# One 128x64 product for four heads' chunk states, four copies of its diagonal blocks, and a reordered projection

## The reference, cut to what matters

```python
def step(carry, inp):
    z, s = carry
    u_t, dt_t, k_t, Bz_t, Bx_t, Cz_t, Cx_t = inp
    dtE = dt_t[:, :, None, None]
    S = 1.0 / (1.0 + dt_t[..., None] * k_t[..., None] + (dt_t * dt_t)[..., None] * A)
    z = S[..., None] * (z - dtE * A[None, :, :, None] * s + dtE * (Bz_t[..., None] * u_t[:, :, None, :]))
    s = s + dtE * z + dtE * (Bx_t[..., None] * u_t[:, :, None, :])
    y = jnp.einsum('bhn,bhnd->bhd', Cz_t, z) + jnp.einsum('bhn,bhnd->bhd', Cx_t, s)
    return ((z, s), y)
```

## Time and profile before

| | us |
|---|---|
| median of 3 runs | 2338.43 (2335.57 to 2339.53) |
| profiled execution | 2331.21 |
| its span, first to last instruction | 2329.6 |
| VectorE busy in the span | 2050.5 (88%) |
| TensorE busy in the span | 1875.7 (81%) |
| ScalarE busy in the span | 1083.9 (47%) |

### The profile page before, as it was taken

The page is one execution under the profiler, slowest core; times in us unless marked ns, Lnnn a source line. Parts: engine busy times, 40 slices in busy tenths (PEclk is TensorE's granted clock), DMA queues, the critical chain, the costliest instruction groups (busy, mean ns, idle before and its releaser), DMA issues. The chain is left out here.

```text
span 2329.6 us, 78341 instructions
## 1 busy us (share of the span) xinstructions
PE 1875.7 (81%) x31266; PEld 1078.5 (46%) x31266; DVE 2050.5 (88%) x5467; ACT 1083.9 (47%) x1700; POOL 84.5 (4%) x28
## 2 busy tenths in 40 slices
PE   6777468987888898888888889887888898367886
PEld 3333134444444444444444444444444444246775
DVE  6887599999999999999989989998999998487774
ACT  4665235454444454445544444544545455034553
POOL 0000000000000000000000000000000000153300
PEclk9898779999999999999999999999999999578997
DMA  4555634655555565545655554665455543433400
GB/s 139 178 214 184 178 92 112 147 134 131 124 127 125 119 150 130 125 106 134 145 123 126 138 124 109 145 143 125 110 126 129 117 113 87 159 154 136 145 27 27
DMA packets 224663, 300.25 MB, mean 129 GB/s; under 512 B 96784, under 2 KB 114192, under 8 KB 218128
## 3 DMA queue, kind: packets, MB, share of 16 engines
q1 hardware_dynamic: 174416, 212.11, 35.9%
q10 hardware_dynamic: 48704, 78.68, 13.3%
q0 software_dynamic: 1152, 4.19, 0.5%
HBM read 240.85 MB, written 50.86 MB: 125 GB/s over the span
## 5 line engine op out<-in xcount | busy, mean ns | idle before, releaser
L670 PE MATMUL m_ps_a<-m_valT,m_w_bc 128*128 128x512 f32 x2048 | 962.1, 619 | 59.8 <-DMA m_valT<-scratch_valT 32.0
L670 PEld LDWEIGHTS m_ps_a<-m_valT,m_w_bc 128*128 128x128 f32 x2048 | 389.8, 198 | 491.1 <-issue 483.7
L958 DVE TENSOR_TENSOR m_prod<-m_psi,m_shear 128x128 f32<-128x128 f32 x960 | 369.0, 384 | 0.0
L962 DVE TENSOR_TENSOR m_psi<-m_psi,m_prod 128x128 f32<-128x128 f32 x960 | 368.4, 384 | 0.0
L818 ACT ACTIVATE m_sq<-m_ps_a 128x512 f32<-128x512 f32 x256 | 152.8, 597 | 372.4 <-PE m_ps_a L670 367.9
L833 ACT ACTIVATE m_kT<-m_ps_g 128x512 f32<-128x512 f32 x128 | 72.0, 596 | 249.8 <-PE m_ps_g L716 249.8
L716 PE MATMUL m_ps_g<-m_ident,m_k 128*128 128x128 f32 x512 | 88.9, 330 | 103.8 <-DVE m_k L1060 103.5
L695 PE MATMUL m_ps_g<-m_q,m_k 32*64 32x64 f32 x8192 | 122.8, 232 | 45.3 <-issue 38.9
L695 PEld LDWEIGHTS m_ps_g<-m_q,m_k 32*64 32x64 f32 x8192 | 107.5, 133 | 100.2 <-ACT m_dX L840 53.3
L819 ACT ACTIVATE m_raw<-m_ps_a 128x512 f32<-128x512 f32 x256 | 151.6, 592 | 0.0
L755 PEld LDWEIGHTS m_ps_y<-m_q,m_X 32*16 32x16 f32 x7168 | 105.2, 94 | 84.1 <-issue 84.1
(11 more groups left out here) (143 smaller groups left out, 3061.7 us busy)
## 6 DMA issues: line engine op xcount, KB each, us to landing
m_scale<-scratch_norm SPq DMA_DIRECT2D x256, 256.0 KB, 5.3
m_w_bc<-in_w_bcT ACTq DMA_DIRECT2D x252, 256.0 KB, 4.7
m_shear<-scratch_n_alpha SPq DMA_DIRECT2D x64, 256.0 KB, 5.3
m_shear<-scratch_beta SPq DMA_DIRECT2D x256, 64.0 KB, 4.1
m_det<-scratch_gd SPq DMA_DIRECT2D x256, 64.0 KB, 4.5
scratch_gateT<-gate SPq DMA_DIRECT2D x8, 1024.0 KB, 3.9
scratch_valT<-val SPq DMA_DIRECT2D x8, 1024.0 KB, 4.5
scratch_svgT<-svg SPq DMA_DIRECT2D x8, 1024.0 KB, 5.5
```

What stands on the lines that cost most here:

```text
L670: mm = pe.matmul(ps_a[j % 2].ap(), w_bc[:, j, kt, :], valT[:, kt, :], start=(kt == 0), stop=(kt == KI - 1), skip_group_check=True)
L958: dve.tensor_tensor(prod.ap(), psi_t[half][:, :, :, :, t], shear_t[half][:, :, :, t].unsqueeze(1).to_broadcast([P, 2, 2, HALF * NC]), ALU. ...
L962: ins = dve.tensor_tensor(psi_t[half][:, :, :, :, t + 1], psi_t[half][:, :, :, :, t], prod[:, :, ::-1, :], ALU.add)
```

## The change

The chunk states of four heads are made by one product per chunk and part: 128 columns of kT (all four heads' states) against 64 columns of u (all four heads' values). The result is 128x64, of which the four 32x16 blocks on the diagonal are the heads' states. All 8 chunks are made instead of 7. They lie in the upper half of all four banks of `ps_g` (`place`: even chunks in banks 0 and 2, odd ones in 1 and 3). ScalarE takes the blocks out with four copies, one for each head's 32 partitions, over four banks. `dX` holds the chunks in the order of `place`. In `inner`, product 0 stands whole ahead of the chunk states, and product 1 stands between them and the scores.

```diff
@@ -458,7 +458,7 @@
         kt = sb("kt", [P, 2, T])
         g = sb("g", [P, HP, PAIRS * C])
         kT = sb("kT", [P, 2, T])
-        dX = sb("dX", [P, NC - 1, 2, DH])
+        dX = sb("dX", [P, NC, 2, DH])
         X = sb("X", [P, NC - 1, 2, DH])
         cross = sb("cross", [P, 2, 2, DH])
         V = sb("V", [P, 2, DH])
@@ -470,11 +470,14 @@
         ps_g = ctx.enter_context(nc.psum_tensor("m_ps_g", [P, HP, T], F32))
         ps_y = ps("y")
 
-        def ps_dX(c):
-
-            col = PAIRS * C + c // 2 * 2 * DH
-            return ps_g[:, 2 + c % 2, col:col + 2 * DH].rearrange("p (r d) -> p r d", r=2)
-
+        def place(c):
+
+            return (c // 4 * 2 + c % 2) * 2 + c // 2 % 2
+
+        def ps_dX(c, part):
+
+            bank, col = place(c) // 2, PAIRS * C + (place(c) % 2 * 2 + part) * HP * DH
+            return ps_g[:, bank, col:col + HP * DH]
 
         consts_in = sem("consts_in")
         const_set = sem("const_set")
@@ -698,13 +701,11 @@
                         mm.then_inc(g_made.sem, g_made.step)
 
                 def chunk_states(s, c):
+
                     for part in range(2):
-                        for h in range(HP):
-                            heads = slice(c // 2 * P + h * N, c // 2 * P + (h + 1) * N)
-                            mm = pe.matmul(ps_dX(c)[h * N:(h + 1) * N, part, :], kT[rows_of(c), part, heads],
-                                           u[rows_of(c), s, c // 2, h * DH:(h + 1) * DH], start=True, stop=True,
-                                           skip_group_check=True)
-                    if c == NC - 2:
+                        mm = pe.matmul(ps_dX(c, part), kT[rows_of(c), part, c // 2 * P:(c // 2 + 1) * P],
+                                       u[rows_of(c), s, c // 2, :], start=True, stop=True, skip_group_check=True)
+                    if c == NC - 1:
                         mm.then_inc(dX_made.sem, dX_made.step)
 
                 def transpose_k(b, group):
@@ -721,20 +722,19 @@
 
                     s = group % 2
                     if ahead:
-                        product(b, group + 2, 0, (0, 1, 2))
+                        product(b, group + 2, 0, range(KI))
                     pe.wait_ge(kT_ready.sem, kT_ready.at(b, group * 2 + 1))
                     pe.wait_ge(u_in[s].sem, u_in[s].at(b, group // 2))
                     pe.sem_inc(passed, 1)
-                    for c in range(NC - 1):
+                    for c in range(NC):
                         chunk_states(s, c)
                     if ahead:
-                        product(b, group + 2, 0, (3,))
+                        product(b, group + 2, 1, range(KI))
                     pe.wait_ge(dX_ready.sem, dX_ready.at(b, group))
                     pe.wait_ge(q_ready.sem, q_ready.at(b, group))
                     for c in range(NC):
                         scores(s, c)
                     if ahead:
-                        product(b, group + 2, 1, range(KI))
                         product(b, group + 2, 2, range(KI))
 
                 def inner_outputs(s, odd):
@@ -835,11 +835,11 @@
                 def copy_dX(b, group):
                     act.wait_ge(dX_made.sem, dX_made.at(b, group))
                     act.wait_ge(X_ready.sem, X_ready.at(b, group * (NC - 1) - 1))
-                    for odd in range(2):
-                        count = NC // 2 - odd
-                        ins = act.activation(dX[:, odd:NC - 1:2].rearrange("p c r d -> p c (r d)"),
-                                             ps_g[:, 2 + odd, PAIRS * C:PAIRS * C + count * 2 * DH
-                                                  ].rearrange("p (c e) -> p c e", c=count), ACT.Copy)
+                    for h in range(HP):
+                        rows, cols = slice(h * N, (h + 1) * N), slice(h * DH, (h + 1) * DH)
+                        ins = act.activation(dX[rows].rearrange("p (k i) r d -> p k (i r) d", k=HP),
+                                             ps_g[rows, :, PAIRS * C:].rearrange("p k (i c) -> p k i c", i=HP)[:, :, :, cols],
+                                             ACT.Copy)
                     ins.then_inc(dX_ready.sem, dX_ready.step)
 
                 def store_y(b, group):
@@ -1095,7 +1095,7 @@
                         dve.wait_ge(y_made.sem, y_made.at(b, group - 1))
                         for c in range(NC - 1):
                             if c:
-                                dve.tensor_tensor(V.ap(), dX[:, c], X[:, c - 1], ALU.add).then_inc(own.sem, own.one())
+                                dve.tensor_tensor(V.ap(), dX[:, place(c)], X[:, c - 1], ALU.add).then_inc(own.sem, own.one())
                                 v_made = own.n
                                 advance(1)
                                 dve.wait_ge(own.sem, v_made)
```

## The result

| | before | after |
|---|---|---|
| median of the runs, us | 2337.0 (4 runs) | 2500.19 (2495.32 to 2504.69, 4 runs) |
| ratio, 95% interval | | 1.0698 (1.0668 to 1.0728) |
| span of the profiled execution, us | 2329.6 | 2494.5 |
| mean granted TensorE clock | 0.913 | 0.888 |

What follows compares the result with a forecast made beforehand. VectorE, in program order, was taken to bound the kernel; dX 4.03 us later per group gave 89 + 136 us, less 10 and 15, plus 10: +210 us, so 2548 us, range 2440 to 2640.

Steps and rivals of the forecast that it cites:

- one-for-one rule: First m_cross on VectorE: each microsecond dX comes later than VectorE is ready costs the kernel one, once per group.
- Rival E: First m_cross: the change doesn't reach VectorE because slack grows with the period; about 2338 us, chance 0.03.
- Product 0 whole in front: TensorE ahead of the chunk states: its last quarter, two records, delays dX by 0.86 us, double at half clock.
- The chunk states: TensorE: 32 records paced by 128-column weight loads take 3.5 us instead of 1.13, so dX comes 2.37 us later.
- rival D: Chunk states: both row halves side by side, 1.1 us, and TensorE keeps full clock; kernel faster, 2300 us, chance 0.04.
- its own sign of being wrong: The prediction called itself wrong if chunk states took 2 us or less, or VectorE didn't wait at first m_cross.
- Rival A: Chunk states: the 64 moving columns set the pace in single file, 2.1 us; 2458 us, chance 0.10.
- C: Chunk states: weight load and product in turn on the same rows, 5.5 us; 2676 us, chance 0.08.
- B: Chunk states: only starts of products cost, so 32 records take about 0.5 us; 2361 us, chance 0.05.
- The copies: ScalarE's copies of dX: four of 384 ns, overlapping by 0.10 us, take 1.22 us, 0.80 us more than before.
- The clock: TensorE at group start: longer waits for k make more groups start at half clock, plus 10 us in all.
- L1036: First product of a group on VectorE, 49.7 us idle: the new wait covers 15 us; 29.5 of "issue" stay.

Runs made afterwards that it cites:

- e3: Changed kernel with two dX copies of all 128 partitions instead of four of 32 (states of heads 1 to 3 left wrong): 2429.85 us, ratio 1.0388.
- e2: Kernel before with only the new order: product 0 whole ahead of the old chunk states, product 1 between them and the scores: 2389.27 us, ratio 1.0201.
- e1: Changed kernel with the chunk states of all even chunks first, then the odd ones, instead of alternating: 2575.55 us, ratio 1.1001.
- e8: Changed kernel with eight dX copies instead of four, each head's 32 partitions twice with two banks each time: 2521.9 us, one run.
- e4: Changed kernel plus eight unused identity products on TensorE between a group's last output and the wait for the next k: 2449.33 us, ratio 1.0452.
- e6: Changed kernel with one quarter of product 0 ahead of the chunk states, three before the scores, product 1 after them: 2373.65 us, ratio 1.0075.
- e7: Kernel before with only the first quarter of product 0 ahead of its chunk states, the other three before the scores: 2347.93 us, ratio 0.9972.

## Why the prediction was right, step by step

**The bound and the one-for-one rule: right.** VectorE's wait for dX was forecast at some 230 us in nearly all groups, with ScalarE's copy as releaser; it is 220.4 us in all 64. e3 bears the rule out (1.09 us less of copying, 1.1 us a group less in time), and so do the periods: from the k that ends at 733.98 to the next at 761.00 lie 27.02 us, the 25.7 of a group without a wait plus its wait of 1.29. Over the groups after, the period less the wait for dX has a median of 25.7 us, as before the change. Rival E is out.

**Product 0 whole in front: the term was right** (0.86 forecast, 4.52 − 3.66 = 0.86 measured). That the order alone costs 2.0% [e2] was not foreseen as a separate sum.

**The chunk states: over-sized, and the reason is shown.** 3.5 us was forecast, 2.05 measured, so the step adds 0.92 us and not 2.37. The price of a weight load was about right: within one half of the rows a record starts every 0.112 us, near the 0.118 of the earlier trace rows. What failed was the overlap given to alternating chunks: the prediction let only one load hide at each change of chunk, and took "both halves side by side" for the unlikely rival D. They do run side by side, at the price of their loads, and that halves the time a record. 2.05 us lies just above the 2 us that the prediction named as its own sign of being wrong. Rival A had nearly the right number (2.1 us) for a wrong reason, as e1 shows; A's time of 2458 us came out too low because of the copies and the clock. C, load and product in turn, would need over 5 us for one half after the other; e1 took 3.39. The Trainium skill, "TensorE: Matmul & The Clock Gate", section "The mechanism", says that a weight load overlaps a running product only where the row group differs. The traces don't agree: on the same rows a record with its own load starts every 0.112 us, though one such load lasts 0.188. B, fixed costs, is out too: the 16 products take longer than the 56, 2.05 against 1.13 us. The Trainium skill, "TensorEngine Tiling (Array Packing)", section "Instruction Overhead", puts some 60 cycles of overhead on every matmul. By that rule fewer products would shorten the step; the trace doesn't agree, it grew.

**The copies: under-sized.** 1.22 us was forecast from overlaps of 0.10 us (4 × 0.384 − 3 × 0.10 is 1.24); the duration was right (384 forecast, 375 ns measured) but there is no overlap where the partitions change [e8]: 1.54 us, +1.12 instead of +0.80.

**The clock: under-sized, and by luck it made the number come out.** With the measured sizes the lateness at full clock is 0.86 + 0.92 + 1.12 = 2.90 us, not 4.03. By the prediction's own sum that is 22 × 2.90 + 42 × 2.10 − 10 − 15 = 127 us, and the kernel took 163. With the 39.8 us that L1036 gave back in place of 15 the sum is 102, so some 61 us are left for half clock and late starts. The prediction gave 10 us to more groups at half clock; the number of such groups rose from 22 to 52. Taken by itself, a full-clock group that starts on time waits 1.3 us, 83 us over 64 groups; the other 137 us of waits come with half clock and with TensorE's late starts. e4 shows the clock's part as a cause, of some 51 us net of the filler's own cost. So the forecast of 2548 came near by luck, since its errors partly cancel: the states 1.45 us a group too dear (93 us over 64 groups), the copies 0.32 too cheap, the clock much too cheap.

**L1036: right in direction, under-sized.** 15 us were taken back in the sum, 39.8 in fact. The 29.5 us marked "issue", which I took for fixed, fell to 5.3 with the others, so most of that behaves like a wait that a later group start covers; which one, the runs don't tell.

**Scores and masks: right.** The scores end at 745.8, VectorE takes them at 750.60, and TensorE's wait for dX ahead of the scores is gone in all but two groups.

**The parts, in points of the ratio.** The new order +2.0 on the kernel before [e2]; the copies +3.1 [after against e3]; the rest, wide products and an eighth chunk, +1.9 [e3 against e2]. They are not independent: with the states early, everything new together costs 0.75 against before [e6], or 1.1 against e7 with its states as early, since most of it then lies inside VectorE's 7 us.

## What to carry to other kernels

Find the engine that works in order and is busy all the time, and measure, per iteration, how early each thing arrives that it waits for: here 2.9 us of lateness a group against 0.8 us of slack, with the half clock that followed, became 7% of the time, and moving the same work ahead of a filler product brought nearly all of it back. Work that is moved ahead of a producer counts like a slower producer, also when it hides a later wait on its own engine. When the bounding engine waits longer, the engines behind it stand longer too, and a TensorE that stands can come back at half clock on the very chain that is waited for, here in 52 of 64 groups instead of 22; price that loop, too.

## What the runs showed of the hardware

- Products on rows 0 to 63 and on rows 64 to 127 with 128-column weights run side by side when they alternate: 32 records in 2.05 us, against 3.39 with one half after the other [after, e1]; within one half a record starts every 0.112 us.
- On ScalarE a copy from PSUM starts up to 0.1 us before the one ahead has ended if both use the same partitions (0.17 us from start to start at 0.26 us each), and only after its end when the partitions differ (0.26; 0.39 for copies of 0.375).
- Eight unused products on TensorE a group made a kernel 2.3% faster (1.0452 against 1.0698 of before; 2449.33 against 2500.19 us), with a granted clock of 0.97 instead of 0.91 over the mix stage.
